# A fused attention and feed-forward block: the middle job of a unit moved behind the value product

## What is computed

```python
scores = einsum('bhqd,bhkd->bhqk', q, k) * scale + bias      # 16 heads of 8, 1024 x 1024 per head
attn   = softmax(scores, axis=-1)
ctx    = einsum('bhqk,bhkd->bhqd', attn, v)                   # then @ Wo + bo

xq, wq = fp4_quant_dequant(x), fp4_quant_dequant(w)           # blocks of 16, grid 0, .5, 1, 1.5, 2, 3, 4, 6
h      = silu(fp4_linear(x, w_gate)) * fp4_linear(x, w_up)    # 128 -> 352
ffn    = fp4_linear(h, w_down)                                # 352 -> 128
```

## Time and profile before

| what | us |
|---|---|
| median of 3 runs | 824.98 (824.71 to 826.10) |
| the profiled execution's own time | 827.07 |
| its span | 825.2 |
| busy: PE, DVE, ACT, POOL | 742.4, 733.4, 665.6, 415.0 |
| share of the span: PE, DVE, ACT, POOL | 90%, 89%, 81%, 50% |

### The profile page before, as it was taken

How to read it: one execution, slowest core, us unless ns; L and a number is a source line. 1 busy time by engine, 2 the same in 40 slices (tenths; PEclk the granted TensorE clock), 3 DMA queues, 4 the chain that set the end, 5 groups by cost and what they waited for, 6 DMA issues and landing times.

```text
span 825.2 us, 14500 instructions
## 1 busy us (share of the span) xinstructions
PE 742.4 (90%) x4939; PEld 221.1 (27%) x4939; DVE 733.4 (89%) x1338; ACT 665.6 (81%) x1372; POOL 415.0 (50%) x411
## 2 busy tenths in 40 slices
PE   3198999989899999989899999989899999898987
PEld 2011232222232333223132333222232332222223
DVE  8698999999989989899999999999999899999931
ACT  4203988888788988888898989888888889898996
POOL 6447245473536646483545564671634561362551
PEclk9655999999999999999999999999999999999999
DMA  5730001023102002050100102140100100000000
GB/s 149 230 80 2 2 2 54 26 77 78 40 2 41 15 2 77 14 152 5 40 2 4 38 2 91 53 116 2 40 2 2 40 27 2 2 2 2 2 2 26
DMA packets 32848, 31.87 MB, mean 39 GB/s; under 512 B 4360, under 2 KB 26568, under 8 KB 32776
## 3 DMA queue, kind: packets, MB, share of 16 engines
q1 hardware_dynamic: 32776, 30.96, 13.5%
HBM read 15.91 MB, written 15.04 MB: 38 GB/s over the span
## 4 chain that ended last, share of the span: by engine, by line
PE 60%; DVE 26%; ACT 4%; POOL 3%; issue 3%; DMA 2%; SPq 1%; POOLq 0%; ACTq 0%; DVEq 0%
PE mx L1105 22%; PE pv L1133 22%; DVE neg_half L966 20%; PE low L1171 3%; ACT probs L755 3%; PE low L1156 3%; PE low L1150 2%; PE low L1182 2%; PE low L1163 2%; DVE am L935 1%; PE low L1092 1%; DVE ctx_s L987 1%; DVE mb L955 1%; PE low L1144 1%; PE low L1197 1%
## 5 line engine op out<-in xcount | busy, mean ns | idle before, releaser
L966 DVE TENSOR_REDUCE neg_half<-mx 128x1 f32<-128x512 f32 x1024 | 643.8, 681 | 50.5 <-PE mx L1105 43.9
L755 ACT ACTIVATE probs<-low 128x512 f32<-128x512 f32 x1005 | 551.8, 614 | 78.4 <-PE low L1122 67.1
L1105 PE MATMUL mx<-k_op,q_op 51*128 51x512 bf16 x1024 | 335.9, 395 | 58.3 <-DVE neg_half L966 36.7
L1122 PE MATMUL low<-q_op,k_op 53*128 53x512 bf16 x1005 | 316.2, 385 | 0.8 <-DMA q_op<-m_rows 0.8
L1133 PE MATMUL pv<-probs,v_op 128*32 128x512 f32 x2048 | 273.6, 606 | 3.1 <-ACT pv_s L855 1.4
L1105 PEld LDWEIGHTS mx<-k_op,q_op 51*128 51x128 bf16 x1024 | 71.9, 94 | 365.0 <-DVE neg_half L966 298.6
L657 POOL CAST neg_parts<-neg_max 128x16 bf16<-128x16 f32 x31 | 6.8, 220 | 156.0 <-DVE neg_max L972 66.9
L564 POOL TENSOR_SCALAR mb<-mb 128x960 f32<-128x960 f32 (+2 forms) x17 | 58.7, 3456 | 27.2 <-DVE mb L955 25.8
L1122 PEld LDWEIGHTS low<-q_op,k_op 53*128 53x128 bf16 x1005 | 69.0, 93 | 7.6 <-ACT probs L755 5.3
L1133 PEld LDWEIGHTS pv<-probs,v_op 128*32 128x32 f32 x2048 | 40.3, 108 | 88.8 <-ACT probs L755 37.8
L553 POOL TENSOR_TENSOR zb<-hid,inv 128x704 f32<-128x704 f32 x16 | 22.2, 1386 | 54.5 <-DVE inv L950 53.8
(11 more groups left out here) (143 smaller groups left out, 627.6 us busy)
## 6 DMA issues: line engine op xcount, KB each, us to landing
q_op<-q_rows SPq DMA_DIRECT2D x32, 192.0 KB, 3.7
k_op<-k_rows SPq DMA_DIRECT2D x32, 192.0 KB, 4.7
q_rows<-qp SPq DMA_DIRECT2D x8, 384.0 KB, 2.6
k_rows<-kp SPq DMA_DIRECT2D x8, 384.0 KB, 3.0
x_s<-in_L_attn_inputs_dram SPq DMA_DIRECT2D x8, 256.0 KB, 3.6
q_rows<-qp SPq DMA_DIRECT2D x8, 256.0 KB, 2.9
k_rows<-kp SPq DMA_DIRECT2D x8, 256.0 KB, 3.3
out_dram<-o_s SPq DMA_DIRECT2D x7, 256.0 KB, 3.1
```

The costliest lines, as they stand in the source:

```text
L755: nc.scalar.activation(probs[U % 3][:, 2 * g + x, :], bank("exp", U, j), ACT.Exp).then_inc(st_free, 1)
L966: nc.vector.tensor_reduce(neg_half[m % 2][:, i + kh:i + kh + 1], slot("max", pos, kh), AX.X, ALU.max, negate=True).then_inc(mx_free, 1)
L1105: nc.tensor.matmul(slot("max", pos, kh), q, k, start=True, stop=True).then_inc(mx_full, 1)
L1122: nc.tensor.matmul(bank("exp", U, j), k_op[quad][r, g, kt * P:(kt + 1) * P], q_op[quad][r, g, half * HALF:(half + 1) * HALF], start=True, ...
```

## The change

The middle job of a unit moves from between the two halves to behind the value product, ahead of the end job. So a unit is now four pairs of maximum and score, the value product, the middle job, the end job. ScalarE empties the middle job's bank behind exponential 3 instead of behind exponential 1, and `rings()` follows, so that the order in the shared banks is exponentials 0 to 3, middle, end. On VectorE the two kinds of middle job that it takes part in ("bvo", and the last "wo") come behind the reduction of half 1 instead of ahead of it. No instruction is added or removed, and no count of banks or slots changes.

```diff
@@ rings() @@
-            for job in middle(U) if i == 0 else ():
+            for job in middle(U) if i == 1 else ():
                 to_ring(job)
@@ scalar @@
-                    for job in middle(U) if j == 1 else ():
+                    for job in middle(U) if j == 3 else ():
                         job_on_scalar(job)
@@ vector @@
+                    if pos < CHUNKS:
+                        reduce_chunk(pos)
                     for job in middle(U) if i == 1 else ():
                         if job[0] in IN_DVE_RING:
                             job_on_vector(job)
                         elif job[0:2] == ("wo", NG - 1):
                             add_last_wo(job[1], job[2])
-                    if pos < CHUNKS:
-                        reduce_chunk(pos)
```

## The result

The changed kernel takes 902.31 us (median of 4 runs, 899.84 to 903.29) where the kernel before takes 824.85 beside it. The ratio is 1.093, with an interval of 1.091 to 1.095: slower by 77 us.

The account below looks back on a forecast made before the run. Middle-job units were taken as bound by TensorE, the others by a loop of TensorE and VectorE through three mx slots. +77.7 - 10.7 = +67.0, plus 5 for the copy, made +72 on 825.0: 897 us, range 872 to 914.

Parts of the forecast that it names:

- What bounds a unit: Middle-job units: TensorE, 2.07 us + job; after the change, a loop through TensorE and VectorE, 2.49 + job.
- (a): Gap in TensorE's burst: the fourth maximum waits for VectorE; +0.42 us in each of 185 units, +77.7 us.
- (c): VectorE's extra work: mostly hidden in the job's length in the 185 units; -10.7 us, leaving +67.0 us.
- (b): Switches on TensorE's array: one bfloat16/float32 change fewer, 0.09 us per unit, already in 2.49, only lengthening TensorE's wait.
- (d): Value product waits for ScalarE's copy of pv: 0.16 us in 25 more units, 4 us; taken as +5 us.
- (e): ScalarE's banks: emptied in time, so nothing; if late, up to 9 us in the 32 gate units.
- What would show it: Signs: fourth maximum at 1.17 us; TensorE's waits 37 to about 80 us, VectorE's 44 to 100 or more; busy times, tail unchanged.
- The rivals: Four other outcomes: faster (chance 0.04), slower by half (0.05), the same within 0.2% (0.01), slower still (0.05).
- the faster one: TensorE sets the end and VectorE's queue covers value product and job: 17 us less, 808 us; chance 0.04.
- The half-way one: VectorE's backlog lets half of the units escape the pause: 34 us + 5, 864 us; chance 0.05.
- a tenth of the units: Slower still: TensorE's clock drops to 1.2 GHz there, 38 us; with late ScalarE banks 930 to 945 us; chance 0.05.

Follow-up runs that it names:

- Experiments 1: The changed kernel with the middle job behind the third pair of maximum and score instead of behind the value product: 834.78 us, ratio 1.011.
- experiment 2: The changed kernel with the middle job behind four pairs but ahead of the value product, on TensorE only: 896.26 us, ratio 1.085.
- 3: Both kernels with each maximum reduced over the last 256 of its 512 scores only: 780.21 us for before, 821.33 for after.
- Experiment 7: The changed kernel, two separate runs: turn ahead of the middle job, 897.93 us; ScalarE's copy of pv ahead of exponential 0, 891.52 us.
- Experiments 4: The changed kernel with four slots for maxima and three banks for scores and jobs: 898.76 us, ratio 1.090.
- 5: The changed kernel with each unit's fourth maximum behind the value product and ahead of the middle job, on TensorE only: 892.07 us, ratio 1.080.
- 6: The kernel before with only the 63 gate and up jobs moved behind the value product: 852.42 us, ratio 1.033.

## Why the prediction was right

Forecast: slower, 897 us (872 to 914). Measured: 902.3. Step by step:

- **What bounds a unit** (2.07 + job, against 2.49 + job behind four maxima): right. Gate and up units take 3.28 us and down units 3.35, as worked out, and the nine units with a lone pvT are unchanged (3.08 in four of them, more where VectorE has extra work, before and after alike). Experiments 1 and 2 place the step between the third and the fourth maximum, and 3 shows the reduction in it.
- **(a), (c), +67.0 us:** 67, that is 74.1 less 5.5 for the copy, 2.8 for the turns and 2.0 for the clock, and 3.2 more for what pvT gave back. The 60 units without a middle job stayed within 0.5 us in sum. What sticks out over the bare loops (worked out with the forecast's own job lengths) was 19 us in these 60 units and 16.5 in the 185 others before; after, it is 18 and, without the four terms just named, some 7.5. So the total fell by 10, as forecast, but not "nearly all" of the rest lies in the 60: extra work of VectorE still shows in units with a job. Two slips of the working change nothing: VectorE's extra work is 667.5 less 607.6, 59.9 and not 61, and the upper ends of the terms add up to 915, not 914.
- **(b):** 0.09 per unit is hidden in the wait. But there was another side: where pvT stands directly behind a middle job, the two take 0.15 less than 2.49 and their lengths give (gate and pvT: 3.72, not 3.87), 3.2 us in 21 units. In experiment 2, with the value product between the two, such a unit takes 3.87. Why is not shown; float32 behind float32 is not enough, as the value product is float32 too.
- **The turn**, whose new neighbour was priced at nothing, is the term that was missed. A turn adds 0.04 us to a gate unit of the kernel before, behind the value product, and 0.23 to one of the kernel after, behind the gate job: 0.16 from the turn to the next maximum, and 0.07 by which the fourth maximum comes later. There VectorE has just collected the maxima (L972), and its first reduction starts 0.49 after its matmul, not 0.42; why is open. Experiment 7 takes 2.8 us back by changing the order of the two.
- **(d), +5 us:** 5.5 in the traces with and without the copy ahead.
- **(e):** right for the kernel after, since 1.17 leaves ScalarE time for every bank. Experiments 4 and 5 show how near it was: with one bank less, or the fourth maximum out of the way, ScalarE's banks and copy bind.
- **What would show it:** TensorE's waits grew to 94 us (some 80 said), VectorE's to 131 (100 or more said); the tail stayed within 1 us, and so did the engines' busy times within 1%, but for the 14 us of TensorE told above.
- **The rivals:** the faster one fails, for the value product and job outlast three results: in the gate unit above VectorE has run dry and stands 0.87. The half-way one would have shown units that escape; of the 48 gate and up units without an end job 35 take 3.28 us and none takes less. The clock fell in two stretches of 3.4 us, some 2 us in all, not in a tenth of the units.
- **Luck in the number:** on the spans the forecast was +72 us and 75.7 came. What it left out comes to 6.9 (turns 2.8, clock 2.0, start and tail 1.6, copy 0.5), of which the 3.2 of pvT, left out too, takes back nearly half. The range would have held either way.

## What to carry to other kernels

Count how many results a producer issues in a row and compare with the slots between it and its consumer. In this kernel the burst was one longer than the ring, and the consumer was through with the full ring (1.86 us) before the producer came back (1.74 us and the job). Then the consumer's first step and everything behind the burst are one serial loop, and each piece of other work adds its whole length. The other work was cheaper inside the burst, at a place where the ring would be full, than behind it. Before a slot is taken from another ring, look at that ring's own burst: here the wait only moved there.

## What was not expected of the hardware

- **VectorE beside GpSimd.** A two-operand product of VectorE took 1.75 to 2.10 us instead of 0.29 while GpSimd ran a two-operand product of 2.23 us, six times in the kernel with pvT as a middle job (mean 643 ns over 32, against 396 in the kernel before, where two of them took 1.24 and 1.33 in the same way). Beside GpSimd's product with one tensor operand (L564, 3.42 us) it kept its 0.29. The Trainium skill, page "GPSIMD Engine Reference", section "1. Specifications", states that the SBUF interfaces are shared with VectorE, with contention for VectorE's instructions with two SBUF inputs; this trace agrees, the product that suffered being one, while the reductions, which read PSUM, kept their mean of 681 ns.
- **The clock after short waits, in some executions.** In the kernel after, the granted clock fell from 2.4 to 1.2 GHz for 3.4 us at 384.4 us, after three waits of 0.6, 0.2 and 0.6 us of TensorE:

```profile
382.55 0.39 PE L1105 MATMUL mx<-k_op,q_op 51*128 51x512 bf16 x1 [0.61 <-DVE neg_half L966]
...
384.11 0.39 PE L1105 MATMUL mx<-k_op,q_op 51*128 51x512 bf16 x1 [0.57 <-DVE neg_half L966]
...
384.43 1.94 PE L1133 MATMUL pv<-probs,v_op 128*32 128x512 f32 x8
```

The value product took 1.9 us instead of 1.0. It is no rule that such waits cost the clock. The same unit has the same three waits in the kernel before, where the full clock stayed:

```profile
353.69 0.39 PE L1105 MATMUL mx<-k_op,q_op 51*128 51x512 bf16 x1 [0.60 <-DVE neg_half L966]
...
355.24 0.39 PE L1105 MATMUL mx<-k_op,q_op 51*128 51x512 bf16 x1 [0.57 <-DVE neg_half L966]
...
355.56 1.06 PE L1133 MATMUL pv<-probs,v_op 128*32 128x512 f32 x8
```

It has them in nine of the kept traces; in three (the kernel after, experiments 2 and 6) the clock fell behind them, and in six, with the copy first and with the turn first among them, it did not, and the unit was 0.9 us shorter. What decides it is not shown. The units that wait 0.35 us in 3.3 kept the full clock throughout the profile of the kernel after.
